# Layer 1 scores of two rows issued together in every other step of TensorE

## The chip, the cores and the metric

The kernel runs on one core of a Trainium2 chip. Every time is in microseconds (us) on the device. The figure of a kernel is the median of several runs; the traces come from one further execution that the hardware profiler recorded.

## The reference

The input `x` is a stack of 128 graphs ("rows" below, since the code calls their index a row), each of 128 nodes by 512 features, with one 128 x 128 boolean adjacency matrix per row. Two graph layers follow one another. Layer 0 has eight heads of 64 and cosine gating; the change does not touch it. Layer 1 is masked attention with four heads of 64:

```
h    = relu(layernorm(x))
q, k, v = h @ Wq, h @ Wk, h @ Wv            # 512 -> 256, four heads of 64
sim  = einsum(q, k) * 64 ** -0.5            # per row and head: 128 x 128
sim  = where(adj, sim, -largest float)
attn = softmax(sim)
out  = einsum(attn, v)                      # back to 128 x 256
x    = x + out @ Wo + bo                    # 256 -> 512
```

## The kernel before, in words

Each engine runs its own instruction list, written out by hand, and the lists meet through semaphores. A row or a group of four rows (`QUAD`) is the unit. Layer 0 ends near 1800 us of the trace and layer 1 takes the rest.

In layer 1 the products that need more precision are made from float16 pairs (a high and a low part): `split_products` issues three matmuls for each 128-deep slice of the contraction, all of them on the whole 128 x 128 array. A "step" is one pass of TensorE's loop over `n`, from 0 to 123. It holds, in this order:

- `project_qk(n + 4)`: 12 matmuls of 512 columns into `ps_pj[0]`, for a quarter of the Q and K of the next group of four rows;
- `project_out(n - 4)`: 6 matmuls of 512 columns into `ps_o`, for the output of row n - 4;
- `scores(n + 1)`: the four heads of row n + 1. Each head has 64 rows of contraction, and two heads stand in the upper and the lower half of the array (`rows = slice(DH * b, DH * b + DH)`). Operands are float32, so each of the four `matmul` calls becomes two hardware matmuls: 8 of 128 columns. They write `ps_s`, a PSUM tensor of two banks of 512 float32; before the change only columns 0 to 255 of each bank are used;
- `project_v(n + 4)`: 12 matmuls of 256 columns;
- `weigh_values(n - 2)`: 12 matmuls of 128 columns that use 64 columns of the array each.

Three further steps (n = 124 to 126) have scores, output projection and value weighting alone, and a tail finishes the last rows.

The other engines follow the same rows. VectorE, in its pass `n`: `add_residual(n - 4)` (L1447, waits for `project_out`), `row_max(n + 1)` (L124 through `mask_scores`: waits for the scores, adds the mask, writes `probs` and the row's maximum `negmax`), `stats`, `normalise(n + 1)` (L1427, L1429), `v_low` (L1416), `aT_low` (L1439), `p_low(n + 1)` (L1434). ScalarE, in its pass `n`: `qk_copy(n + 4)` (L1350 or L1352, reads `ps_pj[0]` when `project_qk` is done), `relu` (L1338), `h_high` (L1343), `exps(n + 1)` (L1364, waits for `negmax`), `v_high` (L1358), `aT_high` (L1376), `p_high(n + 1)` (L1371, waits for `normalise`). SyncE issues the transposing and loading DMAs, and GpSimd makes layer-norm factors, the low part of h and the bias sum; neither list is changed.

Two waits of `scores` matter. Since `ps_s` has a single place for one row, `scores(n)` waits until the maxima of row n - 1 have been taken (`negmax_done`). And for the first row of a group (n a multiple of 4) it waits for the last Q and K copies of that group (`q_done`, `k_done`), the last of which is made from the `project_qk` of the same step.

Of the kernel before, what the change touches and what calls it, by code (L numbers as in the profile page):

```python
# [17 lines left out]
P = 128  # L18
B, D = 128, 512
KT = D // P  # L20
QUAD = 4
# [31 lines left out]
def count(n):  # L53

    return BASE + n
# [30 lines left out]
def row_stats(nc, dve, x, st, bn_done, first):  # L86

    nc.vector.bn_stats(st[:, 0:6], x).then_inc(bn_done, 1)
    dve.wait_ge(bn_done, first + 1)
    nc.vector.bn_aggr(st[:, 6:8], st[:, 0:6]).then_inc(bn_done, 1)  # L90
# [29 lines left out]
def mask_scores(nc, dve, s_ready, n, masked, scores, mask, negmax):  # L120

    dve.wait_ge(s_ready, n)
    for i in range(HB):
        last = nc.vector.tensor_tensor_reduce(masked[:, i], scores[:, i // 2, (i % 2) * P:(i % 2 + 1) * P], mask, -1.0,  # L124
                                              FLOAT_MAX, ALU.add, ALU.min, negmax[:, i:i + 1])
    return last
# [1024 lines left out]
def layer1(nc, prepared, x1, adj, bo, out):  # L1151


    with ExitStack() as ctx:
        def sb(name, shape, dt=F32):
            return ctx.enter_context(nc.sbuf_tensor("l1_" + name, shape, dt))
# [4 lines left out]
        def sem(name):  # L1161
            return ctx.enter_context(nc.semaphore("l1_" + name))
# [3 lines left out]
        q_sb, k_sb, v_hi, v_lo, hT = (prepared[name] for name in ("q_sb", "k_sb", "v_hi", "v_lo", "hT"))  # L1166
# [6 lines left out]
        mask_u8, mask = prepared["mask_u8"], prepared["mask"]  # L1173
# [3 lines left out]
        probs = sb("probs", [P, HB, P])  # L1177
# [9 lines left out]
        ps_s = ctx.enter_context(nc.psum_tensor("l1_ps_s", [P, 2, 512], F32))  # L1187
# [12 lines left out]
        qk_ready, vp_ready, s_ready, av_ready, o_ready = pe_sems = [  # L1200
            sem(n) for n in ("qk_ready", "vp_ready", "s_ready", "av_ready", "o_ready")]
        relu_done, hhi_done, q_done, k_done, vhi_done, exp_done, phi_done, ahi_done = act_sems = [
            sem(n) for n in ("relu_done", "hhi_done", "q_done", "k_done", "vhi_done", "exp_done", "phi_done", "ahi_done")]
        hlo_done, vlo_done, negmax_done, rec_done, np_done, plo_done, alo_done, out_done = dve_sems = [
            sem(n) for n in ("hlo_done", "vlo_done", "negmax_done", "rec_done", "np_done", "plo_done", "alo_done", "out_done")]
# [6 lines left out]
        def row(i):  # L1212

            return xg[:, i - MADE] if MADE <= i < HELD else ring[:, i % RING]

        def row_loaded(i):

            return x_loaded[i % (2 * QUAD)], 16 * ((i - HELD) // (2 * QUAD) + 1)
# [183 lines left out]
        @block.vector  # L1402
        def _(dve):
            for s, made in ((bn_done, 2 * HELD), (hlo_done, MADE), (vlo_done, QUAD), (negmax_done, 0), (rec_done, 0), (np_done, 0),
                            (plo_done, 0), (alo_done, 0), (out_done, 0)):
                dve.sem_inc(s, count(made))

            def stats(i):
                loaded, value = row_loaded(i)
                dve.wait_ge(loaded, value)  # L1410
                row_stats(nc, dve, row(i), ln_st[:, i % (2 * QUAD)], bn_done, count(2 * i))

            def v_low(i):
                dve.wait_ge(vhi_done, count(i + 1))
                at = (slice(None), i // QUAD % 2, i % QUAD)
                nc.vector.tensor_tensor(v_lo[at], ps_pj[1][:, 0:INNER], v_hi[at], ALU.subtract).then_inc(vlo_done, 1)  # L1416

            def row_max(n):
                if n % QUAD == 0:
                    dve.wait_ge(mask_ready, count(n // QUAD + 1))  # L1420
                dve.wait_ge(np_done, count(n))
                mask_scores(nc, dve, s_ready, count(n + 1), probs, ps_s, mask[:, n // QUAD % 2, n % QUAD],
                            negmax[:, n % 2]).then_inc(negmax_done, 1)

            def normalise(n):
                dve.wait_ge(exp_done, count(n + 1))
                nc.vector.reciprocal(rec[:], zsum[:, n % 2]).then_inc(rec_done, 1)  # L1427
                dve.wait_ge(rec_done, count(n + 1))
                nc.vector.tensor_tensor(nprobs[:], probs[:], rec[:].unsqueeze(2).to_broadcast([P, HB, P]),  # L1429
                                        ALU.mult).then_inc(np_done, 1)  # L1430

            def p_low(n):
                dve.wait_ge(phi_done, count(n + 1))
                nc.vector.scalar_tensor_tensor(p16[:, n % 2, 1], nprobs[:], F16_SCALE, p16[:, n % 2, 0], ALU.mult,  # L1434
                                               ALU.subtract).then_inc(plo_done, 1)

            def aT_low(n):
                dve.wait_ge(ahi_done, count(n + 1))
                nc.vector.scalar_tensor_tensor(aT_lo[:, n % 2], ps_av[n % 2][:, 0:PAIRS1 * P].rearrange("p (k n) -> p k n", k=PAIRS1),  # L1439
                                               1.0 / F16_SCALE, aT_hi[:, n % 2], ALU.mult, ALU.subtract).then_inc(alo_done, 1)  # L1440

            def add_residual(n):
                dve.wait_ge(o_ready, count(n + 1))
                dve.wait_ge(res_ready, count(n + 1))
                if n >= 4:
                    dve.wait_ge(out_stored[n % 4], 16 * (n // 4))
                nc.vector.scalar_tensor_tensor(out_sb[:, n % 4], ps_o[n % 2][:], unscale["o"], xres[:, n % 4], ALU.mult,  # L1447
                                               ALU.add).then_inc(out_done, 1)

            row_max(0)  # L1450
            normalise(0)
            p_low(0)
            for i in range(HELD, 15):
                stats(i)
            for n in range(B - QUAD):
                if n >= 4:
                    add_residual(n - 4)
                row_max(n + 1)
                if n + 15 < B:
                    stats(n + 15)  # L1460
                normalise(n + 1)
                v_low(n + QUAD)
                if n >= 2:
                    aT_low(n - 2)
                p_low(n + 1)
            row_max(B - 3)
            for n in range(B - QUAD, B - 1):
                add_residual(n - 4)
                normalise(n + 1)
                if n + 2 < B:  # L1470
                    row_max(n + 2)
                p_low(n + 1)
                aT_low(n - 2)
            for i in range(B - 5, B - 2):
                add_residual(i)
                aT_low(i + 2)
            add_residual(B - 2)
            add_residual(B - 1)

        @block.tensor  # L1480
        def _(pe):
# [22 lines left out]
                split_products(nc.tensor, ps_pj[1][:, 0:INNER], lambda k: hT[:, g % 2, k, cols], lambda k: hT[:, g % 2, KT + k, cols],  # L1504
                               lambda k: w_hi["v"][:, k, :], lambda k: w_lo["v"][:, k, :], KT).then_inc(vp_ready, 1)

            def scores(n):
                g, j = divmod(n, QUAD)
                cols = slice(j * P, (j + 1) * P)
                if j == 0:  # L1510
                    pe.wait_ge(q_done, count(2 * g + 2))
                    pe.wait_ge(k_done, count(2 * g + 2))
                pe.wait_ge(negmax_done, count(n))
                for pr in range(PAIRS1):
                    for b in range(2):
                        rows = slice(DH * b, DH * b + DH)
                        mm = nc.tensor.matmul(ps_s[:, b, pr * P:(pr + 1) * P], q_sb[rows, g % 2, pr, cols], k_sb[rows, g % 2, pr, cols],  # L1517
                                              start=True, stop=True)
                mm.then_inc(s_ready, 1)

# [14 lines left out]
            def project_out(n):  # L1535
                pe.wait_ge(alo_done, count(n + 1))
                pe.wait_ge(out_done, count(n - 1))
                split_products(nc.tensor, ps_o[n % 2][:], lambda k: aT_hi[:, n % 2, k, :], lambda k: aT_lo[:, n % 2, k, :],
                               lambda k: w_hi["o"][:, k, :], lambda k: w_lo["o"][:, k, :], PAIRS1).then_inc(o_ready, 1)

            scores(0)
            for n in range(B - QUAD):
                project_qk(n + QUAD)
                if n >= 4:
                    project_out(n - 4)
                scores(n + 1)
                project_v(n + QUAD)
                if n >= 2:
                    weigh_values(n - 2)
            for n in range(B - QUAD, B - 1):  # L1550
                scores(n + 1)
                project_out(n - 4)
                weigh_values(n - 2)
            project_out(B - 5)
# [71 lines left out]
```

## Time and profile before

| what | value |
|---|---|
| median of 3 runs | 2648.26 us (2646.65 to 2649.66) |
| profiled execution, its own time | 2644.7 us |
| its span | 2642.9 us |
| mean granted TensorE clock | 0.996 |
| TensorE matmuls, busy | 2584.8 us, 98% of the span |
| VectorE, ScalarE, GpSimd, busy | 1991.5, 1754.2, 1400.6 us |

"Busy" counts the time in which an instruction of the engine was in flight. The profiled execution has a time of its own, 3.6 us under the median of the three runs; the sums are made in it and then set beside the median. A chain of waits follows the work that ended last back through the engines; a timeline lists instructions in order of start, with neighbours of one kind merged: start, time from the first's start to the last's end, and how many.

### The profile page before, as it was taken

What the parts mean: (1) busy time and instruction counts of PE and PEld (TensorE: products, weight loads), DVE (VectorE), ACT (ScalarE), POOL (GpSimd) and SP (SyncE); (2) the same over time, 40 slices, a digit from 0 to 9 for tenths busy, and PEclk for the clock granted to TensorE, in tenths of its full rate; (3) what the DMA queues carried; (4) which work ended last, traced back from release to release, by engine and by line L of the source; (5) the groups of instructions that cost most, each with busy time, mean ns of one, the idle gap of its engine ahead of it and who ended that gap; (6) DMA issues with size and microseconds to landing.
All of it is one profiled execution on the core that took longest, in us unless ns stands there. A gap on an engine that the chain in (4) does not pass through costs nothing. (4 is left out here: it accounts for less than half of the span.)

```text
span 2642.9 us, 62516 instructions
## 1 busy us (share of the span) xinstructions
PE 2584.8 (98%) x20882; PEld 1392.6 (53%) x20886; DVE 1991.5 (75%) x6361; ACT 1754.2 (66%) x5020; POOL 1400.6 (53%) x2790
## 2 busy tenths in 40 slices
PE   7999999999999999999999999997999999999998
PEld 3455555555555555555555555554555555555554
DVE  6577777777877777777777777786777777777766
ACT  3566666666666666666666666675777777777774
POOL 5254455455554555455545554544565656565552
PEclk9999999999999999999999999998999999999999
DMA  4367676666676667767676676678787777778764
GB/s 142 74 150 157 131 143 142 143 150 131 140 151 142 132 136 149 150 131 138 145 148 136 132 145 151 139 149 191 155 175 162 168 165 168 164 162 169 161 148 104
DMA packets 945488, 387.43 MB, mean 147 GB/s; under 512 B 857616, under 2 KB 859152, under 8 KB 945168
## 3 DMA queue, kind: packets, MB, share of 16 engines
q1 hardware_dynamic: 945168, 383.44, 68.5%
q8 instruction: 167, 2.74, 0.4%
q14 instruction: 153, 1.25, 0.2%
HBM read 114.86 MB, written 67.11 MB: 69 GB/s over the span
## 5 line engine op out<-in xcount | busy, mean ns | idle before, releaser
L552 ACT ACTIVATE probs<-probs,negmax 128x128 f32<-128x128 f32 x1024 | 398.2, 390 | 455.0 <-DVE negmax L124 455.0
L465 POOL TENSOR_TENSOR o_sb<-o_sb,xres 128x512 f32<-128x512 f32 x127 | 161.4, 1271 | 498.3 <-DVE o_sb L744 494.9
L166 PE MATMUL l_ps_pj<-hT,room 128*128 128x512 f16 x1488 | 345.3, 382 | 3.0 <-ACT room L1350 3.0
L166 PE MATMUL ps_pj<-wm_hi,hT 128*128 128x512 f16 x1024 | 325.2, 379 | 4.1 <-DVE m_sb L687 3.8
L166 PE MATMUL ps_pj<-wv_hi,hT 128*128 128x512 f16 x1024 | 326.4, 380 | 0.0
L166 PE MATMUL ps_pj<-hT,wk_hi 128*128 128x512 f16 x1024 | 305.9, 380 | 0.9 <-DVE wk_lo L766 0.9
L166 PE MATMUL ps_pj<-hT,wq_hi 128*128 128x512 f16 x1024 | 304.5, 379 | 0.0
L1364 ACT ACTIVATE l_probs<-l_probs,l_negmax 128x128 f32<-128x128 f32 x512 | 199.2, 390 | 139.5 <-DVE l_negmax L124 139.4
L1299 POOL TENSOR_TENSOR l_h<-l_h 128x512 f16<-128x512 f32 x120 | 139.6, 1164 | 282.1 <-DVE l_out_sb L1447 244.9
L124 DVE CUSTOM_DVE_ANT_0 probs<-ps_sc,mask 128x128 f32<-128x128 f32 x1024 | 235.2, 284 | 46.9 <-PE ps_sc L986 46.3
L726 DVE SCALAR_TENSOR_TENSOR c<-cprobs,c 128x512 f16<-128x512 f32 x256 | 185.3, 724 | 79.6 <-ACT c L559 79.1
L559 ACT ACTIVATE c<-cprobs 128x512 f16<-128x512 f32 x256 | 160.2, 626 | 118.3 <-DVE cprobs L720 116.0
L166 PEld LDWEIGHTS l_ps_pj<-hT,room 128*128 128x128 f16 x1488 | 136.2, 98 | 162.9 <-issue 3.7
L682 DVE TENSOR_TENSOR h<-h 128x512 f16<-128x512 f32 x136 | 114.9, 845 | 116.5 <-ACT h L518 116.2
L720 DVE SCALAR_TENSOR_TENSOR cprobs<-ps_sc,bound,probs 128x512 f32<-128x512 f32 x256 | 188.9, 738 | 12.6 <-ACT probs L552 9.5
L166 PE MATMUL ps_pj<-hT,wk_lo 128*128 128x512 f16 x512 | 194.0, 379 | 0.0
L166 PE MATMUL ps_pj<-wv_lo,hT 128*128 128x512 f16 x512 | 194.0, 379 | 0.0
L166 PE MATMUL ps_pj<-hT,wq_lo 128*128 128x512 f16 x512 | 194.0, 379 | 0.0
L166 PE MATMUL ps_pj<-wm_lo,hT 128*128 128x512 f16 x512 | 194.0, 379 | 0.0
L1310 POOL TENSOR_TENSOR l_xres<-l_ring,l_bo_rows 128x512 f32<-128x512 f32 x124 | 171.0, 1380 | 40.7 <-DVE l_out_sb L1447 40.7
L552 ACT ACTIVATION_READ_ACCUMULATOR probs<-probs,negmax 128x1 f32 x1024 | 191.1, 187 | 0.0
L979 PEld LDWEIGHTS ps_sc<-room 64*128 64x128 f32 x2048 | 134.1, 186 | 107.0 <-issue 106.7
(172 smaller groups left out, 6197.2 us busy)
## 6 DMA issues: line engine op xcount, KB each, us to landing
xg<-in_x SPq DMA_DIRECT2D x128, 256.0 KB, 3.5
xres<-in_x SPq DMA_DIRECT2D x128, 256.0 KB, 3.2
x_scratch<-o_sb SPq DMA_DIRECT2D x128, 256.0 KB, 2.4
out<-l_out_sb SPq DMA_DIRECT2D x128, 256.0 KB, 3.3
l_ring<-x_scratch SPq DMA_DIRECT2D x124, 256.0 KB, 3.2
mask_u<-in_adj SPq DMA_DIRECT2D x64, 64.0 KB, 2.6
cpT<-c SPq DMA_TRANSPOSE x256, 3.2
xg<-x_scratch SPq DMA_DIRECT2D x12, 256.0 KB, 3.7
```

The costliest lines, as they stand in the source:

```text
L124: last = nc.vector.tensor_tensor_reduce(masked[:, i], scores[:, i // 2, (i % 2) * P:(i % 2 + 1) * P], mask, -1.0, FLOAT_MAX, ALU.add, ALU. ...
L166: last = pe.matmul(out, a(kt), b(kt), start=(n == 0), stop=(n == 3 * kts - 1))
L465: nc.gpsimd.tensor_tensor(o_sb[:, j % 2], o_sb[:, j % 2], xres[:, j % 2], ALU.add).then_inc(res_done, 1)
L552: last = nc.scalar.activation(probs[:, i], probs[:, i], ACT.Exp, bias=negmax[:, u % 2, i:i + 1], scale=-1.0, accum_out=zsum[:, u % 4, hh:h ...
L559: nc.scalar.activation(c16[:, n % 2, 0], cprobs[:], ACT.Copy, scale=F16_SCALE).then_inc(cph_done, 1)
L682: nc.vector.tensor_tensor(h16[:, j % 2, D:], h32[:, j % 2], h16[:, j % 2, 0:D], ALU.subtract).then_inc(hlo_done, 1)
L720: nc.vector.scalar_tensor_tensor(cprobs[:].rearrange("p (b h) n -> p b (h n)", b=2), ps_c[n % 2], bound[:, t % 2, j:j + 1], probs[:].rearr ...
L726: nc.vector.scalar_tensor_tensor(c16[:, n % 2, 1], cprobs[:], F16_SCALE, c16[:, n % 2, 0], ALU.mult, ALU.subtract).then_inc(cpl_done, 1)
L979: nc.tensor.matmul(ps_s[n % 2][:, b, pl * P:(pl + 1) * P], q_sb[rows, t % 2, pr, cols], k_sb[rows, t % 2, pr, cols], start=True, stop=True)
L1299: nc.gpsimd.tensor_tensor(h16[:, i % 2, D:], h32[:, i % 2], h16[:, i % 2, 0:D], ALU.subtract).then_inc(hlo_done, 1)
L1310: nc.gpsimd.tensor_tensor(xres[:, i % 4], row(i), bo_rows[:], ALU.add).then_inc(res_ready, 1)
L1364: last = nc.scalar.activation(probs[:, hh], probs[:, hh], ACT.Exp, bias=negmax[:, n % 2, hh:hh + 1], scale=-1.0, accum_out=zsum[:, n % 2, ...
```

## The change

In the steps with odd n, `scores(n + 1)` and `scores(n + 2)` are issued one after the other. The steps with even n (0 excepted) have no scores. Odd rows write the columns 256 to 511 of both banks, even rows the columns 0 to 255. The second row of a pair waits for the same maxima as the first (`count(n - 1)` in place of `count(n)`), so both rows wait until every older row has been read. On VectorE, `row_max` reads the half that belongs to its row; for the even row of a pair it waits until the scores of both rows are done, so that TensorE is not writing a bank that VectorE reads. Rows 2 and 3, 4 and 5, up to 124 and 125 are paired: 62 pairs. Rows 0, 1, 126 and 127 stay single.

```diff
@@ VectorE, row_max
                 dve.wait_ge(np_done, count(n))
-                mask_scores(nc, dve, s_ready, count(n + 1), probs, ps_s, mask[:, n // QUAD % 2, n % QUAD],
+                paired = n % 2 == 0 and 2 <= n < B - 2
+                mask_scores(nc, dve, s_ready, count(n + 2 if paired else n + 1), probs, ps_s[:, :, n % 2 * 2 * P:(n % 2 + 1) * 2 * P],
+                            mask[:, n // QUAD % 2, n % QUAD],
                             negmax[:, n % 2]).then_inc(negmax_done, 1)
@@ TensorE, scores
-            def scores(n):
+            def scores(n, second=False):
...
-                pe.wait_ge(negmax_done, count(n))
+                pe.wait_ge(negmax_done, count(n if not second else n - 1))
                 for pr in range(PAIRS1):
                     for b in range(2):
                         rows = slice(DH * b, DH * b + DH)
-                        mm = nc.tensor.matmul(ps_s[:, b, pr * P:(pr + 1) * P], q_sb[rows, g % 2, pr, cols], k_sb[rows, g % 2, pr, cols],
+                        first = (2 * (n % 2) + pr) * P
+                        mm = nc.tensor.matmul(ps_s[:, b, first:first + P], q_sb[rows, g % 2, pr, cols], k_sb[rows, g % 2, pr, cols],
                                               start=True, stop=True)
@@ TensorE, the loop over n
                     project_out(n - 4)
-                scores(n + 1)
+                if n == 0:
+                    scores(1)
+                if n % 2:
+                    scores(n + 1)
+                    scores(n + 2, True)
                 project_v(n + QUAD)
...
             for n in range(B - QUAD, B - 1):
-                scores(n + 1)
+                if n > B - QUAD:
+                    scores(n + 1)
                 project_out(n - 4)
                 weigh_values(n - 2)
```

## Rows read from the trace of the kernel before

**Rows 1.** Busy by stretch: PE, PEld, DVE, ACT, POOL us (instructions), granted clock, DMA, GB/s
```profile
1830.40:1833.80 3.40, 3.40 (x20) 2.47 (x20) 1.72 (x10) 2.30 (x8) 2.13 (x2) 0.51 1.03 295
1833.80:1900.00 66.20, 66.20 (x516) 37.16 (x515) 47.59 (x160) 48.24 (x142) 38.16 (x73) 1.00 0.81 171
1900.00:2500.00 600.00, 600.00 (x4607) 337.29 (x4606) 442.23 (x1474) 443.83 (x1294) 353.90 (x600) 1.00 0.78 165
```
**Rows 2.** Chain of waits, 2100 to 2160 us: start, us, what
```profile
by line: PE l_ps_pj L166 63.9%; PE l_ps_o L166 19.4%; PE l_ps_s L1517 9.7%; PE l_ps_av L1530 7.6%
...
2105.39 0.65 PE l_ps_s L1517 x8
...
2111.90 0.65 PE l_ps_s L1517 x8
```
**Rows 3.** Timeline of TensorE, one step
```profile
2101.33 2.76 PE L166 MATMUL l_ps_pj<-hT,room 128*128 128x512 f16 x12
...
2105.01 0.38 PE L166 MATMUL l_ps_o<-room,l_aT_lo 128*128 128x512 f16 x1
2105.32 0.71 PE L1517 MATMUL l_ps_s<-room 64*128 64x128 f32 x8
2105.97 1.49 PE L166 MATMUL l_ps_pj<-room,hT 128*128 128x256 f16 x12
```
**Rows 4.** The scores' tile, 1900 to 2500 us: ns min/median/max of one
```profile
L1517 PE MATMUL l_ps_s<-room x736: 272/272/373, 1903.5 to 2496.3; 64*128 64x128 f32 x184
```
**Rows 5.** Timeline of VectorE, the same step
```profile
2105.43 0.75 DVE L1447 SCALAR_TENSOR_TENSOR l_out_sb<-l_ps_o,l_w_st,l_xres 128x512 f32<-128x512 f32 x1 [0.73 <-PE l_ps_o L166]
2106.19 0.29 DVE L124 CUSTOM_DVE_ANT_0 l_probs<-l_ps_s,mask 128x128 f32<-128x128 f32 x1
...
2109.66 0.42 DVE L1416 TENSOR_TENSOR l_v_lo<-l_ps_pj,l_v_hi 128x256 f16<-128x256 f32 x1
...
2110.44 0.98 DVE L1434 SCALAR_TENSOR_TENSOR l_p<-l_nprobs,l_p 128x512 f16<-128x512 f32 x1
```
**Rows 6.** Timeline of ScalarE, the same step
```profile
2107.16 0.40 ACT L1364 ACTIVATE l_probs<-l_probs,l_negmax 128x128 f32<-128x128 f32 x1 [0.99 <-DVE l_negmax L124]
...
2109.78 0.63 ACT L1371 ACTIVATE l_p<-l_nprobs 128x512 f16<-128x512 f32 x1 [0.44 <-DVE l_nprobs L1429]
2110.64 0.69 ACT L1350 ACTIVATE room<-l_ps_pj,l_w_st 128x512 f32<-128x512 f32 x1 [0.23 <-PE l_ps_pj L166]
```
**Rows 7.** Timeline of ScalarE and TensorE, start of layer 1
```profile
1829.03 0.63 ACT L1371 ACTIVATE l_p<-l_nprobs 128x512 f16<-128x512 f32 x1 [0.96 <-DVE l_nprobs L1429]
1829.57 0.67 ACT L1352 ACTIVATE room<-l_ps_pj,l_w_st 128x512 f32<-128x512 f32 x1
...
1830.34 1.17 PE L1517 MATMUL l_ps_s<-room 64*128 64x128 f32 x8 [2.98 <-issue]
```
**Rows 8.** Waits of all engines, 1900 to 2500 us: total, times, longest
```profile
POOL l_h L1299 <- DVE l_out_sb L1447: 204.4, 66, 4.1
ACT l_probs L1364 <- DVE l_negmax L124: 90.7, 92, 1.3
DVE l_rec L1427 <- ACT l_probs L1364: 83.0, 93, 0.9
DVE l_out_sb L1447 <- PE l_ps_o L166: 63.9, 89, 0.8
```
**Rows 9.** Chain of waits from 2611 us, the end
```profile
2611.79 1.31 PE l_ps_o L166 x6
2613.12 0.71 DVE l_out_sb L1447
...
2613.92 0.29 DVE l_probs L124
```

## The prediction

> **What bounds the kernel now.** I read the busy time by stretch first. From 1833.8 to 2500 us TensorE has a matmul in flight for the whole of both stretches, at a granted clock of 1.00, that is 2.4 GHz, while VectorE and ScalarE are busy for 442 and 444 us of 600 [rows 1]. Busy alone does not prove a bound, so the chain of waits comes next: over sixty microseconds it never leaves TensorE, and its pieces repeat, the scores at 2105.39 and again at 2111.90 [rows 2]. A step is therefore 6.51 us, and it is the sum of what TensorE issues. The waits say the same from the other side: ScalarE waits about 1 us a step for the maxima, VectorE 0.9 for the exponentials and 0.7 for the output projection, GpSimd up to 4 us; the list has no wait of a TensorE matmul on another engine [rows 8]. So in the steady part a microsecond taken from TensorE's list is a microsecond of the kernel, until one of those waits has shrunk to nothing and turns round.
>
> The timeline of one step says what the scores cost there [rows 3]. Twelve matmuls of 512 columns take 2.76 us from first start to last end and one alone 0.38, so they follow each other every (2.76 - 0.38) / 11 = 0.216 us. The last matmul of the output projection starts at 2105.01; the next one of the same kind could start at 2105.23. The V projection instead starts at 2105.97. The block of scores takes 5.97 - 5.23 = 0.74 us of TensorE's time. Little of that is arithmetic. The eight matmuls run from 5.32 to 6.03; the longest rows in the block are 373 ns and the median 272 [rows 4], which I read as the first matmuls having to wait some 0.1 us for their own weights. The first two, one in the upper and one in the lower half, end together at 5.32 + 0.373 = 5.69, and the six others end in the 0.34 us after that: (0.71 - 0.373) / 6 = 0.056 us a matmul, 8 x 0.056 = 0.45 us in all. The other 0.74 - 0.45 = 0.29 us is the way in (0.09 from 5.23 to 5.32, and 0.10 of exposed weights) and the way out (0.10), paid where the array goes from whole-array matmuls to half-array ones and back.
>
> **The change part by part.**
>
> Even steps lose their block. The output projection is followed directly by the V projection, both on the whole array. That takes off 0.74 us: step 5.77.
>
> Odd steps get eight more matmuls in an open block. If they stream as the first eight do they add 0.45 us: step 6.96. Bounds: not under 0.45, since TensorE issues nothing faster in this block; not over 0.74, a whole block with its entry. I take 0.45. The second row uses the same two halves of the array, the same two banks and operands of the same shape; nothing distinguishes its first load from the third load in the block, except that it carries a semaphore wait, and that has been met since `row_max` of the row before. The first output matmul carries waits too, and its group stays in step with its neighbours: 18 matmuls from 2101.33 to 2105.01 are 17 intervals in 3.68 us, 0.216 each [rows 3].
>
> Eight matmuls of 128 columns take 0.45 us in this trace [rows 3, 4], which is the pace I use. The Trainium skill has a price that speaks against the change. The Trainium skill ("TensorE: Matmul & The Clock Gate", Back-to-back issue gap) gives about 81 ns a matmul of 128 columns for a sustained stream of loads and matmuls, against some 56 for isolated ones; by 81 the eight would be 0.65 us, a pair would save 0.09 and the change 5 us (an estimate from that page's figure). This trace agrees with the page's smaller number.
>
> Gain of a pair: 0.74 - 0.45 = 0.29 us, on average 0.147 a step. TensorE becomes the bound with the scores at 1830.34 [rows 7], which are those of row 4, in step 3. From there to the last full step I count 60 odd steps (3 to 121) and 60 even ones (4 to 122): 60 x 0.29 = 17.6 us, from unrounded 0.744 and 0.448, 17.8.
>
> The moved wait on VectorE. In an odd step the even row's `row_max` now waits for sixteen matmuls. Before, it starts at 2106.19, when `add_residual` has just ended (2105.43 + 0.75) [rows 5]; the scores were done at 6.03, so their wait was covered. Now they end 0.45 later, at 6.48, and `row_max` starts near 6.51: 0.33 later than before. Behind it on VectorE stand the statistics, `normalise`, `v_low`, `aT_low` and `p_low`; behind its maxima stand ScalarE's exponentials. Who on TensorE waits for them? The next step's `project_v` waits for `v_low`, which was done 5.07 us after the last output matmul (2109.66 + 0.42 - 2105.01 [rows 3, 5]) and becomes done 5.40 after it, while that `project_v` starts 7.2 after it; `weigh_values` takes the row two steps later. ScalarE's `p_high` moves from 4.77 us after the last output matmul (2109.78 - 2105.01 [rows 3, 6]) to 5.10 after it, but the next `project_qk` of this long step ends 6.0 us after it, so `qk_copy` isn't held. Cost zero in the steady part, hidden under TensorE's own longer step.
>
> In an even step the opposite holds: the odd row's scores have been there for a step, so `row_max` starts when `add_residual` ends, at the same distance from the output projection as before, 1.18 us. But TensorE's step is 0.74 shorter, and here is the tight place. Call X the start of the last output matmul of an even step. `p_high` starts at X + 4.77 as before. `qk_copy` comes behind it; where it does not wait for TensorE it starts 0.54 later, and the scores that wait for it start 1.31 after `p_high` (1829.03 to 1830.34 [rows 7]): X + 6.08. TensorE itself reaches the scores at X + 6.51 - 0.74 + 0.31 = X + 6.08. These meet. The wait exists only where a group starts, once in four steps, 30 times. I take 0.03 us each, 0.9 us together. Bounds: 0 (the copy is in time or its wait is covered by the way in) and 0.3 (9 us, the longest of ScalarE's waits being that much over their mean [rows 8]). All other waits on `qk_copy` are for the next step's projection, 3 us later. The cover that goes is ScalarE's 0.23 us of waiting for `ps_pj` [rows 6].
>
> Other lists. `p_low` is sometimes 0.98 us and ends at 2111.42 [rows 5]; in an odd step after an even one `add_residual` could start at X + 6.18 and VectorE is free at X + 6.41, but `row_max` there waits for the pair until X + 7.3, so this hides as well. SyncE's and GpSimd's instructions are unchanged in number and order; the pace goes from 6.51 to 6.36 us a step, and GpSimd's 204 us of waiting on VectorE [rows 8] covers that. ScalarE is busy 4.8 us a step [rows 1], under even the 5.77.
>
> The start. In steps 1 and 2 of layer 1 TensorE waits for others in either order, and I count nothing. Step 3's scores fall into the stretch with the clock at 0.51, i.e. 1.2 GHz [rows 1], right behind 2.98 us without a matmul [rows 7]; the eight further ones cost twice 0.45 there, 0.45 more than counted.
>
> The end. In step 123 the chain leaves TensorE at the output projection and goes through `add_residual` to the `row_max` of row 124 at 2613.92 [rows 9]. That now waits for the scores of row 125 too: 0.33 us later, not earlier. From there to the end softmax of the last rows follows one behind the other on VectorE and ScalarE, and the removed scores of step 124 are beside it: nothing.
>
> Sum: -17.8 + 0.9 + 0.45 + 0.33 = -16.1 us. The profiled execution's 2644.7 would become 2628.6; it lies 3.6 under the median of the runs, and 2648.3 - 16.1 = 2632.
>
> **The rivals.**
>
> 1. The row boundary costs. The second row's first load isn't hidden, because it stands behind a semaphore wait, or the loads of a longer block fall behind. With 0.10 us of exposed weights once [rows 4] the pair saves 0.19 and the change 60 x 0.1 = 6 us less, 2638; exposed twice, 12 us less, 2644. For it: the load at the start of the block does show. Against it: within the block, loads are hidden, and waits that are already met cost nothing elsewhere [rows 3]. The Trainium skill's 81 ns (the same page and section) would bring the change to 2643, in this rival's range.
>
> 2. ScalarE's copy is late for the group's first scores. Each 0.1 us costs 30 x 0.1 = 3 us. A lateness of 0.2 to 0.3 gives 2637 to 2640. For it: my two times meet within 0.01 us, and both are worked out. Against: nothing else in the chain moves.
>
> 3. Slower. The same chain, `add_residual`, `row_max`, exponentials, `normalise`, `p_high`, `qk_copy`, scores, becomes the bound of the even steps, because in a step with different phases something on ScalarE comes in front of it (the relu and `h_high` of the pass before, held by the later maxima of the odd step). It decides from 0.59 us of lateness in four steps, since two pairs save 0.59. If even steps didn't shorten at all, the odd steps' 0.45 would remain: 60 x 0.45 = 27 us slower, 2675. Against: ScalarE has 1 us of wait in front of its exponentials and 0.44 in front of `p_high` [rows 6], and the odd step gives it half a microsecond more, not less.
>
> 4. The change does not do what it says: the 0.29 us of entry and exit come back in the even step, because the way from the last output matmul to the V projection has a cost that the scores hid now, such as the wait for `v_low`. That gives 2648. `v_low` is done 1.8 us before (5.4 against 7.2, above), so I hold little of it.
>
> **How the numbers follow.** The forecast, 2629 to 2635, has 0.64; rival 1 has 0.12, rival 2 0.10, rival 3 0.05, rival 4 0.05, and 0.04 stays for a gain over 19 us (the waits of the start falling better). The median of other runs can lie a microsecond or two off by itself, as the three runs show. To hold 8 of 10 the range takes the forecast and most of rivals 1 and 2: 2627.5 to 2640. A difference of 0.2%, 5.3 us, is what a measurement of this kernel can tell from none: faster means under 2643, which holds the forecast, rival 2 and nearly all of rival 1, 0.88; within 0.07; slower 0.05.
>
> **What would show it.** In the trace after: blocks of sixteen matmuls of scores that last 0.71 + 0.45 = 1.16 us, with still only the first at 373 ns; the distance from the last output matmul to the V projection 0.22 us in even steps and 1.41 in odd ones; pairs of steps of 12.72 us where there were 13.02; the first exponential of an odd step 0.33 later against the output projection than that of an even one. If scores of every second pair start later than 0.31 us after the last output matmul, with ScalarE's L1352 as the releaser, rival 2 or 3 holds. If sixteen take more than 1.2 us, rival 1 does. The prediction is wrong in its main step if TensorE's chain has an interruption in the steady part at all.

## The result and the profile after

The changed kernel takes 2630.78 us, median of 4 runs (2629.68 to 2631.97), against 2648.83 before (4 runs): a ratio of 0.9936, 95% interval 0.9924 to 0.9948. Run again beside the experiments it took 2630.78 once more, 0.9937 (0.9922 to 0.9952). It is 18.05 us faster by the medians. The two profiled executions differ by less, 2644.7 and 2629.68, 15.0 us, and so do their spans, 2642.9 and 2627.9.

The chain of waits of the kernel after, from 2090 to 2116 us (start, us, what), still stays on TensorE, as in [rows 2], and now has two kinds of step:

```profile
by line: PE l_ps_pj L166 64.5%; PE l_ps_o L166 19.9%; PE l_ps_s L1520 8.4%; PE l_ps_av L1533 7.9%
...
2098.63 1.29 PE l_ps_o L166 x6
2099.93 1.09 PE l_ps_s L1520 x16
2101.02 1.42 PE l_ps_pj L166 x12
...
2105.59 1.29 PE l_ps_o L166 x6
2106.89 1.31 PE l_ps_pj L166 x12
...
2111.35 1.29 PE l_ps_o L166 x6
2112.64 1.09 PE l_ps_s L1520 x16
```

From one block of scores to the next is 2112.64 - 2099.93 = 12.71 us for two steps, where [rows 2] have 2 x 6.51 = 13.02: 0.31 us less a pair. The V projection is shown shorter where no scores precede it, 1.31 against 1.42: with scores ahead of it, the chain charges it the way out of the half-array block. The timeline of TensorE, same place, answers to [rows 3]:

```profile
2099.55 0.38 PE L166 MATMUL l_ps_o<-room,l_aT_lo 128*128 128x512 f16 x1
2099.86 1.16 PE L1520 MATMUL l_ps_s<-room 64*128 64x128 f32 x16
2100.95 1.48 PE L166 MATMUL l_ps_pj<-room,hT 128*128 128x256 f16 x12
...
2106.51 0.38 PE L166 MATMUL l_ps_o<-room,l_aT_lo 128*128 128x512 f16 x1
2106.72 1.47 PE L166 MATMUL l_ps_pj<-room,hT 128*128 128x256 f16 x12
```

Sixteen matmuls take 1.16 us where eight took 0.71, 0.45 more. In the even step the V projection follows the output projection after 0.21 us, where it was 0.96. In the scores' own rows, 1900 to 2500 us, the durations are those of [rows 4], min/median/max:

```profile
L1520 PE MATMUL l_ps_s<-room x752: 272/272/373, 1909.2 to 2494.9; 64*128 64x128 f32 x188
```

The waits of all engines, 1900 to 2500 us, answer to [rows 8]. A line is new, VectorE for the scores, once a pair; and VectorE's wait for the output projection has halved, from 63.9 to 34.2 us. There is no wait of a TensorE matmul on another engine.

```profile
POOL l_h L1299 <- DVE l_out_sb L1449: 110.6, 45, 4.3
ACT l_probs L1364 <- DVE l_negmax L124: 95.5, 94, 1.3
...
DVE l_out_sb L1449 <- PE l_ps_o L166: 34.2, 93, 0.8
DVE l_probs L124 <- PE l_ps_s L1520: 22.3, 47, 0.5
```

**Where the span's 15.0 us come from.** The scores of row 4 start at 1830.34 before and 1831.30 after; those of row 124 at 2613.01 and 2596.09. So the 120 steps between went from 782.67 to 764.79 us, 17.9 less. What lies before them is 0.96 longer, and what follows is 1.9 longer, 31.8 for 29.9.

The 0.96 us need not be the change's. The first scores of layer 1 are already 1.00 later, at 1801.07 for 1800.07, before any pair is issued, and a kernel that issues everything as before (the columns alone, below) has them at 1801.27.

The 1.9 us at the end stand in the chains of waits, before and after:

```profile
2633.14 1.47 PE l_ps_o L166 x6
2634.61 0.46 PE l_ps_av L1530 x12
```
```profile
2616.66 2.74 PE l_ps_o L166 x6
2619.40 0.65 PE l_ps_av L1533 x11
```

From the scores of row 124 to these matmuls it is 20.57 us for 20.13, 0.44 more, and the two groups take 1.27 and 0.19 more: 1.90. They run at half the granted clock, as the busy time by stretch shows (after; columns as in rows 1):

```profile
2612.90:2619.80 6.90, 5.51 (x33) 2.12 (x32) 4.20 (x8) 1.29 (x5) 2.53 (x2) 0.51 0.72 121
2619.80:2627.90 8.10, 4.80 (x38) 2.04 (x34) 3.49 (x6) 0.77 (x2) 0.00 (x0) 1.00 0.50 191
```

There the granted clock is at 1.2 GHz for 6.9 us. Before, the stretch from 2629.2 to 2632.5 is at 0.50 and those beside it at 1.00: 3.3 us, in which the chain is on VectorE and ScalarE, so that they cost it nothing. The longer stretch is not a matter of one execution: a second trace of the changed kernel is at 0.50 from 2613.3 to 2620.0 and has the same 2.74 us, and the trace of the columns alone has 3.3 us at half, as before. Full clock would not give back all of it. The kernel with the other pairs split (below) issues the same matmuls behind row 124 and has full clock there, yet its end is 31.2 us, because a DMA, `l_pT<-l_p`, with 4.43 us in its chain of waits, is then the last to be ready. The columns' kernel ends that way too, after 31.0 us where the kernel before took 29.9, so the end can differ by a microsecond with the issue order unchanged.

### The profile page after: what moved, and what is told of

Its sections match the earlier page's. It is cut to its first block and busy times, and to the rows that moved or that the text cites. A ratio compares the mean times of both kernels' runs of the same rounds, so it can differ in the third digit from the quotient of the medians.

```text
span 2627.9 us, 62516 instructions
## 1 busy us (share of the span) xinstructions
PE 2567.4 (98%) x20882; PEld 1393.0 (53%) x20886; DVE 1987.6 (76%) x6361; ACT 1748.7 (67%) x5020; POOL 1396.8 (53%) x2790
## 3 DMA queue, kind: packets, MB, share of 16 engines
q8 instruction: 167, 2.74, 0.4%
```

## The experiments

Theory 1: the gain is the way into and out of a block in which the array works in halves, paid once for each block. Rivals: the scores being there a step earlier; the columns; and, for what could go wrong, ScalarE's copy before a group's first scores.

**The same change with blocks that aren't joined.**

```diff
                     scores(n + 1)
-                    scores(n + 2, True)
-                project_v(n + QUAD)
+                project_v(n + QUAD, (lambda: scores(n + 2, True)) if n % 2 else None)   # after 6 of its 12 matmuls
...
```

(Left out: `project_v` hands the function on to `split_products`, which calls it halfway.)

> The changed kernel, but the second row of each pair is issued in the middle of the twelve matmuls of the V projection instead of right behind the first row. Everything else of the change stays: the columns, the early second row, VectorE's wait for both rows. Theory 1 (the gain is the way into and out of the half-array block, 0.29 us for each block that is joined to another): 62 blocks become 124 again, the gain is gone, 2646 to 2651 us, and both blocks of an odd step last 0.71 us. Rival (the gain comes from the scores being there a step earlier, so that VectorE and ScalarE run further ahead): the gain stays, about 2631 us.

Measured: 2662.28 us, ratio 1.0058 (1.0042 to 1.0074). The gain is gone, so the rival falls; but it is 11 us over the top of what I expected. Against the changed kernel it is 31.5 us: 62 further blocks at 0.31 us make 19, and waits make the other 12. The chain of waits of this kernel shows both parts:

```profile
2099.90 1.51 PE l_ps_pj L168 x7
2101.41 1.29 PE l_ps_o L168 x6
2102.71 0.38 issue
2103.08 0.71 PE l_ps_s L1522 x8
2103.80 0.76 PE l_ps_pj L168 x6
2104.56 0.65 PE l_ps_s L1522 x8
2105.20 0.76 PE l_ps_pj L168 x6
```

Each block is 0.65 us on the chain, as before the change, and cuts the V projection in two parts of 0.76, whose sum is 0.10 over 1.42. And in front of every second pair, the one that opens a group, is a wait of 0.4 us. About 8 us earlier, in VectorE's and GpSimd's timelines:

```profile
2094.76 1.38 DVE L1433 TENSOR_TENSOR l_nprobs<-l_probs,l_rec 128x512 f32<-128x512 f32 x1
...
2097.45 0.75 DVE L1451 SCALAR_TENSOR_TENSOR l_out_sb<-l_ps_o,l_w_st,l_xres 128x512 f32<-128x512 f32 x1
```
```profile
2094.33 1.26 POOL L1312 TENSOR_TENSOR l_xres<-l_ring,l_bo_rows 128x512 f32<-128x512 f32 x1
```

`normalise` takes 1.38 us instead of 0.69 while GpSimd adds the bias. VectorE is late by that when the output projection is done: `add_residual` starts 0.88 us after the last output matmul (2096.57) instead of 0.42. With it the maxima, the exponentials and ScalarE's copy are late, for which TensorE then waits.

**Doubling the blocks of the kernel before.** Two heads at their place, two in the middle of the V projection:

```diff
-                scores(n + 1)
-                project_v(n + QUAD)
+                scores(n + 1, (0,))
+                project_v(n + QUAD, lambda: scores(n + 1, (1,)))   # after 6 of its 12 matmuls
```

> The kernel before, with the number of blocks doubled: two heads of a row at their place, the other two in the middle of the V projection. The arithmetic is the same. Theory 1: each of some 119 full steps pays the entry and exit once more, 0.29 to 0.31 us, so 35 to 37 us slower than the kernel before, 2683 to 2686 us. Rival (entry and exit are hidden by other work and the gain has another source): within 5 us of the kernel before.

Measured: 2686.12 us, ratio 1.0146 (1.013 to 1.0161), 38.3 us over the 2647.84 of before beside it, at the upper edge of what I expected. Theory 1 holds, 38.3 / 120 = 0.32 us for a further block of the same arithmetic. Its trace gives 0.31: from the scores of row 4 to those of row 124 it takes 817.95 us, and the columns' kernel, also without a half-rate stretch in between, 781.07.

**The columns alone.**

```diff
-                        mm = nc.tensor.matmul(ps_s[:, b, pr * P:(pr + 1) * P],
+                        first = (2 * (n % 2) + pr) * P
+                        mm = nc.tensor.matmul(ps_s[:, b, first:first + P],
```

(VectorE reads the same half, as in the change.)

> The kernel before with the columns alone: odd rows write and read columns 256 to 511 of the two banks, and nothing is issued together. Theory 1: no part of the gain, 2646 to 2651 us. Rival (alternating columns let TensorE or VectorE go faster by itself): faster than 2643 us.

Measured: 2646.94 us, ratio 1.0001 (0.9992 to 1.0011), no part of the gain. The columns are only what makes joining possible.

**The cover of ScalarE's copy taken away.** The pair goes ahead of the output projection in odd steps:

```diff
                 project_qk(n + QUAD)
-                if n >= 4:
-                    project_out(n - 4)
...
                     scores(n + 1)
                     scores(n + 2, True)
+                if n >= 4:
+                    project_out(n - 4)
                 project_v(n + QUAD)
```

> The changed kernel with the pair of scores ahead of the output projection in odd steps, so that the 1.30 us of the output projection no longer cover ScalarE's copy of the last Q and K quarter. If the copy is ready at X + 6.08 (X: start of the last output matmul of an even step) and TensorE reaches the scores at X + 4.8, the first scores of a group wait about 1.3 us, 30 times: 38 us more than the changed kernel, about 2669 us, and scores at the other pairs wait for nothing. Rival (the copy is in truth ready much earlier, so the meeting of the two times that I worked out was wrong): under 0.5 us a group, under 2646 us.

Measured: 2691.25 us, ratio 1.0168 (1.0151 to 1.0185), 60.5 us over the changed kernel where I expected 38. The wait is there at the groups' first scores alone, but it is 1.9 us and not 1.3. Chain of waits of this kernel, then VectorE's and GpSimd's timelines of the step before:

```profile
2103.54 2.70 PE l_ps_pj L166 x12
2106.24 1.91 issue
2108.15 1.16 PE l_ps_s L1520 x16
...
2118.24 2.70 PE l_ps_pj L166 x12
2120.93 1.09 PE l_ps_s L1520 x16
```
```profile
2099.56 1.65 DVE L1431 TENSOR_TENSOR l_nprobs<-l_probs,l_rec 128x512 f32<-128x512 f32 x1
```
```profile
2099.40 1.26 POOL L1310 TENSOR_TENSOR l_xres<-l_ring,l_bo_rows 128x512 f32<-128x512 f32 x1
```

Again `normalise` stands beside GpSimd's addition, and 1.65 - 0.69 = 0.96 us of lateness are enough for the missing 0.6. The last group of this trace is the check: there `normalise` took 0.69 us, and the scores of row 124, at 2657.08, waited 1.12 us. It is not a clean one, since ScalarE and VectorE have no further rows to prepare there. The copy itself was where I had put it: `p_high` at 2106.85, scores at 2108.15, 1.30 later.

**Which half of the split pairs waits.** Only the pairs that open a group are split, or only the others (`n % QUAD == 3` or `== 1` in the line of the first experiment).

> The kernel with split pairs (a_split_pair) came out at 2662 us where 2646 to 2651 was expected, with a wait of 0.44 us before the first scores of most groups; two steps ahead of these waits VectorE's normalise took 1.38 us beside a GpSimd addition in place of 0.69. Here only the pairs that open a group (rows 4g and 4g + 1) are split, 31 of 62; the step after them leads to scores that wait for no copy. Theory (the split costs 0.30 us each and the rest was lateness of ScalarE's copy): 31 x 0.30 = 9 us over the changed kernel, 2640 us. Rival (the split itself costs more than the 0.30 us, whatever follows): half of 31 us more, 2646 us.

> The other half: only the pairs of rows 4g + 2 and 4g + 3 are split. VectorE's late pass is followed by scores that wait for ScalarE's copy. Theory: 9 us for the blocks plus 30 x 0.44 = 13 us of waiting, 2652 to 2654 us, 13 us over the kernel with the group pairs split. Rival (the split itself costs more): the same as that one, 2646 us.

Measured: 2640.32 us, ratio 0.9974 (0.9963 to 0.9985), for the group pairs, as forecast: 31 unjoined blocks cost 9.5 us, 0.31 each. The others: 2643.44 us, ratio 0.9987 (0.9978 to 0.9996), where I expected 2652 to 2654. That is 3 us more and not 13; in its trace the groups' first scores start 0.13 us late and not 0.44, nearly all of them, and the longest `normalise` between 1900 and 2500 us is 1.07 us, where it is 1.39 with all pairs split. The intervals of the two overlap, so by the times the direction is only likely, but 28 waits of 0.13 us make 3.6 us, which fits. With the group pairs split most groups wait for nothing; two do, one by 0.14 us at 2349.01, behind a `normalise` of 1.53 us at 2340.33, and one by 0.41 us at 2580.98, behind one of 1.80 us at 2572.04. So within a kernel the wait goes with the length of the slowed `normalise` about 9 us before it. Between the two kernels it does not: with the group pairs split, one of 1.10 us brings no wait, with the others split one of 1.07 brings 0.13. What else moves there is open. The 0.44 us of the first experiment, in nearly every group, came only with all pairs split.

**The same for the value weighting.**

```diff
-                if n >= 2:
+                if n >= 2 and n % 2 == 0:
                     weigh_values(n - 2)
+                    weigh_values(n - 1)
```

> The changed kernel, with the same done to the value weighting: rows n - 2 and n - 1 one behind the other in even steps, none in odd ones. A block of weighting takes 0.56 us (from the end of the V projection's last matmul to the next projection's first) and its twelve matmuls, in pairs every 0.056 us, 0.34, so each joined pair saves 0.22 us: 60 x 0.22 = 13 us, about 2617 us. Even steps grow to 6.1 us, so ScalarE's copy has 0.3 us of room before the scores. Rival (the earlier second row waits for its transposed probabilities, or the blocks of 64 columns have no such entry cost): 2626 us or more, with waits of the weighting on a DMA or on VectorE.

Measured: 2618.24 us, ratio 0.9891 (0.9876 to 0.9906), 12.5 us under the changed kernel run beside it and 1.2 over the forecast of 2617. Its chain has one block of 0.79 us where there were two of 0.46, and in the odd step, where no weighting stands between them, the V projection and the next Q and K projection take 4.01 us for 1.42 + 2.70:

```profile
2096.73 4.01 PE l_ps_pj L166 x24
...
2102.03 1.31 PE l_ps_pj L166 x12
2103.34 0.79 PE l_ps_av L1533 x24
2104.13 2.70 PE l_ps_pj L166 x12
```

That is 0.24 us a pair by these rows and 12.5 / 60 = 0.21 by the times.

**Scores beside the value weighting.**

```diff
+                project_v(n + QUAD)
                 if n % 2:
                     scores(n + 1)
                     scores(n + 2, True)
-                project_v(n + QUAD)
```

> The changed kernel with the pair of scores moved behind the V projection, next to the value weighting, which also uses the array in parts. If one way between two shapes is as dear as any other, an odd step has three changes of shape in place of four and saves about 0.10 us: 60 x 0.10 = 6 us, about 2625 us. Rival 1 (changing from one partial shape to the other costs as much as leaving and entering the whole array): 2631. Rival 2 (the even row's maxima are 1.3 us later and TensorE waits for VectorE or ScalarE): slower than 2631 us.

Measured: 2625.62 us, ratio 0.9919 (0.9904 to 0.9933), 5.2 us under the changed kernel, as forecast; the intervals overlap. Its chain:

```profile
2107.36 1.31 PE l_ps_pj L166 x12
2108.67 1.09 PE l_ps_s L1520 x16
2109.76 0.46 PE l_ps_av L1533 x12
2110.22 2.70 PE l_ps_pj L166 x12
```

The odd step has lost the longer V projection, 1.42 to 1.31, and nothing has grown: going straight from halves of rows to halves of columns saves one way back to the whole array. Two V projections between 1900 and 2500 us do wait for `v_low`, 1.8 us together in the list of waits, so a little of rival 2 is there.

**Both, and both with V's low part early.** The first moves both kinds of pairs into odd steps (`project_v(n + 4)`, the pair of scores, `weigh_values(n - 2)`, `weigh_values(n - 1)` for odd n). The second adds, on ScalarE and VectorE:

```diff
-                exps(n + 1)
                 v_high(n + QUAD)
+                exps(n + 1)
...
-                normalise(n + 1)
                 v_low(n + QUAD)
+                normalise(n + 1)
```

> Both: pairs of scores and pairs of value weightings in odd steps, side by side behind the V projection; even steps have whole-array matmuls alone. By the sum of the changes of shape it saves 13 + 6 = 19 us against the changed kernel, 2612 us. But even steps shrink to 5.2 us, the low part of V is made 5.5 us after the last output matmul of the even step and the next V projection starts 5.4 after it: a wait of 0.1 to 0.3 us sixty times, 6 to 18 us given back, so 2618 to 2630 us. Which it is tells where the other engines take over as the bound.

> Pairs of scores and of value weightings side by side in odd steps (e_both_in_odd, 2617.4 us), where the V projection of odd steps waited 0.33 us for the low part of V. Here ScalarE's v_high goes ahead of its exponentials and VectorE's v_low ahead of its normalise. If that wait was what the sum missed, it is gone: 55 x 0.33 = 18 us less, about 2600 us, 47 us under the kernel before. Rival (VectorE's and ScalarE's softmax chain is late anyway and the copy of Q and K takes the place of v_low): 2610 us or more.

Measured: 2617.43 us, ratio 0.989 (0.9874 to 0.9907), just under the 2618 to 2630 that I expected, and 2608.86 us, ratio 0.9855 (0.9838 to 0.9871), 9 us over the forecast of 2600 and just under the rival's 2610. In the first, the timelines show the V projection waiting for VectorE:

```profile
2104.97 0.42 DVE L1416 TENSOR_TENSOR l_v_lo<-l_ps_pj,l_v_hi 128x256 f16<-128x256 f32 x1
```
```profile
2104.91 0.38 PE L166 MATMUL l_ps_o<-room,l_aT_lo 128*128 128x512 f16 x1
2105.44 0.83 PE L166 MATMUL l_ps_pj<-room,hT 128*128 128x256 f16 x6 [0.16 <-DVE l_v_lo L1416]
```

The matmul starts 0.53 us after the last output matmul where the stream would give 0.22. The list of waits between 1900 and 2500 us (total, times, longest) has 22 of these where there are 48 odd steps; I had counted one in each:

```profile
PE l_ps_pj L166 <- DVE l_v_lo L1416: 3.5, 22, 0.2
```

Every second odd step waits and the others start at 0.22. That is why the second gains 8.6 us over the first and not 18, and its list has no wait of a TensorE matmul left. It is the fastest kernel of the study, 37 us under the one before and about 22 us under the changed one.

## Why the prediction was right

The measured 2630.8 us stand against a forecast of 2632, and the mechanism is the one forecast, with some of its terms off. That the two lie within 1.2 us is in part luck, as the last point shows.

- **The gain of a pair.** Put at 0.29 us, measured 0.31 (12.71 for 13.02). Eight further matmuls take 0.45 as said; the removed block was worth 0.75 (0.96 - 0.21) and not 0.74. Three kernels give the same price from other sides: 0.32 us a block when blocks are doubled, 0.31 when half of the pairs are split, nothing for the columns. The two stretches measured from row 4 to row 124 differ by 17.9 us; one late start of 0.41 us in the changed kernel is in it (0.34 in the chain below), so 60 pairs gave 18.3 us for the 17.8 forecast. One thing stays open. The block of scores differs from its neighbours in the shape on the array and in its type, float32 beside float16, and no run separates the two. The value weighting, float16 like its neighbours, shows what a change of shape without one of type costs: 0.21 us a block.
- **The row boundary (rival 1).** The sixteen last 1.16 us, which I gave as the sign. The maximum of 373 ns is unchanged and only the first two matmuls of a block have it, so the weights show once a block. The 56 ns that I used hold as a mean. They are not the spacing of single matmuls, though: the matmuls start in pairs, one in each half of the array, and a pair follows a pair after 0.11 us. So the agreement with the smaller of the two figures in the Trainium skill ("TensorE: Matmul & The Clock Gate", Back-to-back issue gap) is one of numbers, and this trace is no test of its 81 ns; it only shows that 0.65 us for eight of these matmuls, the estimate from that figure, would have been wrong, for the 0.45 measured.
- **The moved wait of `row_max`.** Here I misread. I took it that `row_max` had started when `add_residual` ended, that the scores were covered, and that it could start 0.03 us after them. VectorE's timeline after:

```profile
2101.18 0.29 DVE L124 CUSTOM_DVE_ANT_0 l_probs<-l_ps_s,mask 128x128 f32<-128x128 f32 x1 [0.46 <-PE l_ps_s L1520]
...
2106.92 0.75 DVE L1449 SCALAR_TENSOR_TENSOR l_out_sb<-l_ps_o,l_w_st,l_xres 128x512 f32<-128x512 f32 x1 [0.39 <-PE l_ps_o L166]
2107.59 0.28 DVE L124 CUSTOM_DVE_ANT_0 l_probs<-l_ps_s,mask 128x128 f32<-128x128 f32 x1
```

  In the odd step it starts 0.16 us after the last score ends (2099.86 + 1.16 = 2101.02), exactly as in [rows 3, 5] (2106.19 after 2106.03): the scores had been its bound. In the even step, where they are old, it starts 0.67 after the start of `add_residual` instead of 0.76. So in the odd step `row_max` is 0.45 later and not 0.33, and in the even step 0.09 earlier than I had it. Both are hidden as forecast.
- **The copy of Q and K (rival 2).** Forecast: copy and TensorE meet within 0.01 us, 0.03 of wait each, 0.9 together. By the 0.09 us just named it comes in time. One wait is left in the steady part, in the chain of waits, and about 9 us ahead of it VectorE's timeline has the longest `normalise` of the trace:

```profile
2569.03 1.29 PE l_ps_o L166 x6
2570.32 0.34 issue
2570.66 0.34 PE l_ps_s L1520
```
```profile
2561.72 1.80 DVE L1431 TENSOR_TENSOR l_nprobs<-l_probs,l_rec 128x512 f32<-128x512 f32 x1
```

  There `p_high` started at 2569.36 and the scores 1.30 us later, the distance of [rows 7]. The second trace of the changed kernel has the same wait behind the same 1.80 us. That the room is thin is shown by the split pairs too, where half a microsecond of lateness reached TensorE. So the price was too high by about 0.5 us, and the warning right, though the lateness stands behind a `normalise` slowed beside GpSimd, which the prediction did not have.
- **The start.** I added 0.45 us, because eight more matmuls fall into the stretch with the clock at half. They do (the block takes 2.08 us), but the stretch stayed 3.4 us long (1831.3 to 1834.7, at 0.50), and the V projection got out of it in return: 2.15 us for 2.64. From the scores to the first output matmul it is 7.15 us for 6.73, 0.42 more, which is what the eight matmuls cost at full clock. In these two traces the stretch costs half its length, whatever stands in it. The columns' kernel, which has no such stretch there, bears that out: 781.07 us from row 4 to row 124 for 782.67, 1.6 less. That term was wrong, and is nothing.
- **The end.** Forecast 0.33 longer, measured 1.9. Of it 0.44 is `row_max` of row 124, which waits for row 125, and 1.46 are matmuls of the chain that ran at half clock (2.74 us for 1.47, 0.65 for 0.46). I did not foresee that the half-rate stretch would reach them; why it lies there is open.
- **The base.** The sum was -16.1 us. By the traces its terms are -18.3, 0.4, 0 and 1.9, and with the 1.0 before the first pair, for which the prediction has no term, they come to -15.0, the difference of the two profiled executions. The medians differ by 18.05; the 3 us between that and 15.0 are about the spread of single runs, 2.3 to 3.0 us. I carried the 3.6 us between profile and median over to the kernel after; there they were 1.1. So the forecast lies nearer to the median than its terms deserve.

## What to carry to other kernels

Where TensorE is the bound, count the changes of array shape in a step and price them from start-to-start distances: here 0.31 us for a block of half rows, with 4, 8 or 16 matmuls in it, and 0.21 for one of half columns. Joining such blocks pays as long as the results have room to lie side by side and the consumer may wait for the longer block. Before making a step shorter, follow the longest chain of the other engines once around and give its distance to TensorE's need: 0.1 us of room held, but one slowed VectorE instruction used it up. When two releasers of a wait lie within 0.2 us, a timeline doesn't tell which one it was; the kernel in which one of them has moved does.

## What was not expected of the hardware

A VectorE multiplication of 128 x 512 float32 took 1.38 and 1.65 us instead of 0.69 while a GpSimd addition of the same size was running. It hardly moves while the two overlap: in both cases it ended 0.55 us after the addition did (2096.14 after 2095.59, 2101.21 after 2100.66). No run takes the addition away, but in none of the traces is there a `normalise` over 0.76 us without a GpSimd instruction beside it. It was in the trace of before too (1.63 us in the last rows and 1.81 in the steady part), but I read it only as a matter of the end. It set the size of two experiments: 12 us of waits with all pairs split, and 0.6 to 0.8 us a group in the kernel with scores first.

In both kernels the granted clock went to half behind a stretch of about 3 us without a matmul at the start of layer 1 (2.98 us before, 2.96 after). In the last rows it was at half for 3.3 us before and 6.9 after, and so it was in the second traces, 3.3 us with the columns alone and 6.7 with the changed kernel (which had 3.3 more from 2603.0), though the matmuls there are the same but for eight. What half clock costs is where it falls: nothing while the chain is on VectorE and ScalarE, and nearly a doubling, 2.74 us for 1.47, where six output matmuls are in the chain.
